# A selective scan whose reverse input terms come from TensorE instead of GpSimd

## What is computed

```python
def selective_scan(u, delta, A, Bm, Cm, D):
    def step(h, inp):
        u_t, d_t, B_t, C_t = inp
        dA = jnp.exp(d_t[..., None] * A)                       # 128 channels x 16 states
        h = dA * h + (d_t * u_t)[..., None] * B_t[:, None, :]
        y = jnp.einsum('bdn,bn->bd', h, C_t)
        return (h, y)
    ...
def run_bidir(seq, p):
    f = mamba(seq, p)
    r = jnp.flip(mamba(jnp.flip(seq, 1), p), 1)
    return 0.5 * (f + r)
```

## Time and profile before

| | |
|---|---|
| median of 3 runs | 27766.99 us (27764.99 to 27772.45) |
| the profiled execution | 27768.75 us, its span 27767.2 us |
| busy, TensorE (PE) | 18178.2 us, 65% |
| busy, VectorE (DVE) | 25925.0 us, 93% |
| busy, ScalarE (ACT) | 16996.5 us, 61% |
| busy, GpSimd (POOL) | 25520.0 us, 92% |
| DMA queue q1 | 57.9% of 16 engines' span |
| granted TensorE clock, mean | 0.81 |

### The profile page before, as it was taken

How to read it: one execution, slowest core, us unless ns; L and a number is a source line. 1 busy time by engine, 2 the same in 40 slices (tenths; PEclk the granted TensorE clock), 3 DMA queues, 4 the chain that set the end, 5 groups by cost and what they waited for, 6 DMA issues and landing times. The chain is left out here.

```text
span 27767.2 us, 284715 instructions
## 1 busy us (share of the span) xinstructions
PE 18178.2 (65%) x62778; PEld 5277.9 (19%) x62778; DVE 25925.0 (93%) x24107; ACT 16996.5 (61%) x23653; POOL 25520.0 (92%) x11268
## 2 busy tenths in 40 slices
PE   6666666666666666666666666666666666666572
PEld 1111111111111111111111111111111111111120
DVE  8999999999999999999999999999999999999321
ACT  6666666666666666666666666666666666665232
POOL 8999999999999999999999999999999999999000
PEclk8888888888888888888888888888888888887786
DMA  5555555555555555555555555555555555555967
GB/s 189 202 200 202 200 201 199 200 199 199 200 202 200 202 199 201 200 200 200 199 201 201 201 200 200 201 200 200 200 198 202 200 202 201 201 200 183 188 130 180
DMA packets 1914996, 5473.26 MB, mean 197 GB/s; under 512 B 214002, under 2 KB 642818, under 8 KB 1901458
## 3 DMA queue, kind: packets, MB, share of 16 engines
q1 hardware_dynamic: 1912968, 5451.83, 57.9%
HBM read 4644.92 MB, written 805.60 MB: 196 GB/s over the span
## 5 line engine op out<-in xcount | busy, mean ns | idle before, releaser
L796 POOL TENSOR_TENSOR drive<-du_rep,b_rep 128x1024 f32<-128x1024 f32 x8192 | 19201.4, 2389 | 114.5 <-DMA b_rep<-bc_spread 75.1
L729 DVE TENSOR_TENSOR_SCAN decay<-decay,drive 128x512 f32<-128x512 f32 x10752 | 12658.3, 1218 | 132.9 <-issue 54.6
L599 ACT ACTIVATE decay<-delta_rep,a_neg 128x1016 f32<-128x1016 f32 x8192 | 8999.1, 1106 | 598.4 <-DMA delta_rep<-delta_spread 593.6
L453 PE MATMUL y_bank<-read,sel_f 128*32 128x512 f32 x32768 | 5510.3, 805 | 2702.1 <-DVE gated L751 1798.0
L742 DVE TENSOR_TENSOR read<-decay,c_rep 128x1024 f32<-128x1024 f32 (+1 forms) x5632 | 6528.0, 1159 | 0.0
L729 DVE TENSOR_TENSOR_SCAN state<-decay,drive 128x512 f32<-128x512 f32 x5120 | 6203.7, 1212 | 83.8 <-ACT decay L599 81.3
L809 POOL TENSOR_TENSOR read<-state,c_rep 128x1024 f32<-128x1024 f32 x2560 | 6099.0, 2382 | 0.0
L595 ACT COPY decay<-zeros 128x8 f32<-128x8 f32 x5632 | 946.8, 168 | 6807.3 <-DVE read L742 6626.3
L430 PE MATMUL p_bank<-e_one,sel_f 128*128 128x512 f32 x2048 | 1563.5, 854 | 2769.4 <-ACT e_one L580 2487.2
L407 PE MATMUL p_bank<-xt,taps 128*128 128x512 f32 x4096 | 2069.2, 627 | 950.1 <-ACT u L538 492.0
L453 PEld LDWEIGHTS y_bank<-read,sel_f 128*32 128x32 f32 x32768 | 1076.1, 131 | 6474.4 <-issue 4959.4
(11 more groups left out here) (109 smaller groups left out, 14419.8 us busy)
## 6 DMA issues: line engine op xcount, KB each, us to landing
du_rep<-du_spread SPq DMA_DIRECT2D x2048, 512.0 KB, 6.4
delta_rep<-delta_spread SPq DMA_DIRECT2D x2048, 512.0 KB, 6.2
b_rep<-bc_spread SPq DMA_DIRECT2D x2048, 512.0 KB, 7.7
c_rep<-bc_spread SPq DMA_DIRECT2D x2048, 512.0 KB, 4.1
du_spread<-e_log SPq DMA_DIRECT2D x512, 512.0 KB, 2.7
delta_spread<-e_one SPq DMA_DIRECT2D x512, 512.0 KB, 3.6
xt<-in_xs SPq DMA_DIRECT2D x1024, 128.0 KB, 3.4
bc_spread<-bc SPq DMA_DIRECT2D x1024, 64.0 KB, 1.6
```

What stands on the lines that cost most here:

```text
L453: mm = nc.tensor.matmul(y_bank[32 * j:32 * j + 32, :], gather, read[:, (ROW * m + j) % READ_RING, px(d)], start=(m == 0 and d == FWD), sto ...
L599: nc.scalar.activation(inner(place[:, :]), inner(delta_rep[:, j, :]), ACT.Exp, scale=a_neg[s][:, ROW * j + m:ROW * j + m + 1]).then_inc(s_ ...
L729: nc.vector.tensor_tensor_scan(to[:, ::step], decay[place_of(turn, h, q)][:, px(d)][:, ::step], drive[:, q % DRIVE_RING, px(d)][:, ::step] ...
L796: nc.gpsimd.tensor_tensor(drive[:, q % DRIVE_RING, :], du_rep[h][:, j, :], b_rep[:, m, :], ALU.mult).then_inc(s_drive, 1)
```

## The change

The scan of a direction now has its own layout and its own instructions.

- A unit has 16 slots of 1024 columns: eight forward (F) and eight reverse (R), in turn. F slot f covers two channel groups j of one state group m, 512 positions each. R slot r covers 32 channels on the partitions 32g to 32g+31 for four groups g of states, and its columns are (2 sequences, 4 states m, 128 positions); four R slots make one half ("pair") of the sequences.
- The scan of a slot is one VectorE instruction of 1024 columns.
- F drives stay on GpSimd (eight of 1024 columns). R drives are made by TensorE: du is transposed (`turn_du`, step "tr") so that positions lie on the partitions, and is the stationary operand; the moving operand is `b_diag`, a matrix with b of position t in the columns of t and zero elsewhere, so the product gives du[c, t] * b[t, n]. Each drive is one small matmul and 16 matmuls of 64 rows x 32 columns with 256 moving columns. The moving operand is read 4 states at a time out of 16, position by position, and the output has position outermost and m innermost, with 128 elements (512 bytes) between neighbours.
- `b_diag` comes from an image in DRAM whose rows are zeros but for the 16 states in the middle (`store_b_cols`, rows of 64 bytes, from the new step "bt"); reading it with a row step of one row less 16 elements gives the diagonal blocks (`load_diag`).
- R reads (h * C) are all made by GpSimd, in place in `read_r`; VectorE makes 11 and GpSimd 5 of the 16 F reads of a tile.
- ScalarE makes an F decay in two instructions of 508 columns, and the R decays as 16 instructions of 508 columns into SBUF (`decay_r`). A place in PSUM is reused after three slots: a drive of TensorE into one waits for the F read two slots before.
- The p_bank steps are 11 instead of 9, and their places in the unit are new. The sums are four of F and two of R (`sum_r`, 16 matmuls of 256 columns each).

The diff, cut to what sets the work and its order:

```diff
-BY_POOL = (1, 4, 7, 10, 13)
-DRIVE_RING, READ_RING, STATE_RING = 4, 8, 2
+F_OPS = R_OPS = 8
+SLOTS = F_OPS + R_OPS
+WINDOW = 64
+F_BY_POOL = ((1, 5), (1, 4, 7))
+PLACES, DRIVE_RING, F_RING, R_RING = 3, 3, 4, 6
+DRIVE_AHEAD = 2
...
-STEPS = [Step("ds", FWD, 1, 0, 2), Step("ds", REV, 1, 3, 5), Step("bc", 0, 1, 6, 6),
-         Step("x", FWD, 2, 6, 7), Step("x", REV, 2, 7, 8), Step("z", 0, 1, 8, 9),
-         Step("dt", FWD, 2, 9, 10), Step("dt", REV, 2, 10, 11), Step("out", 0, -1, 12, 13)]
+STEPS = [Step("bt", REV, 1, 0, 1), Step("ds", FWD, 1, 1, 2), Step("ds", REV, 1, 3, 4),
+         Step("tr", REV, 1, 7, 7), Step("bc", 0, 1, 7, 8),
+         Step("x", FWD, 2, 8, 9), Step("x", REV, 2, 8, 9), Step("z", 0, 1, 9, 10),
+         Step("dt", FWD, 2, 10, 11), Step("dt", REV, 2, 11, 12), Step("out", 0, -1, 13, 14)]
+DU = {FWD: 3, REV: 6}
+GATE, UD = 5, 7
+R_DECAYS = {0: (4, 5), 1: (6, 7), 2: (8,), 3: (9, 10, 11), 4: (12,), 5: (13, 14, 15)}
+F_SUMS = {6: 0, 8: 1, 12: 2}
+F_SUM_LAST, R_SUM_LAST, R_SUM = 2, 3, 10
...
+            def make_drive(U, i, h, turn, r):          # TensorE
+                to = place[place_of(turn, h, 2 * r + 1)]
+                ti, th, f = before_f(i, h, r)
+                if not (isinstance(ti, int) and ti < 0):
+                    if f in F_BY_POOL[th]:
+                        pe.wait_ge(s_state, F_OPS * U + r)
+                    else:
+                        pe.wait_ge(s_read_v, read_by_vector(ti, th, f) + 1)
...
+                nc.tensor.matmul(to[0:32, 0:NS], du_cols[h][:, 2 * pair, 32 * j:32 * j + 32],
+                                 b_diag[:, pair, 0, 0:NS], start=True, stop=True, tile_position=(0, 0),
+                                 skip_group_check=True)
+                for half in range(2):
+                    for row in range(2):
+                        rows = slice(WINDOW * row, WINDOW * row + WINDOW)
+                        diag = b_diag[rows, pair, half, :].rearrange("p (t n) -> p t n", n=NS)
+                        part = to[:, px(row)].rearrange("p (m t) -> p t m", m=ROW)
+                        part = part[:, WINDOW * half:WINDOW * half + WINDOW, :]
+                        for g in range(4):
+                            mm = nc.tensor.matmul(part[32 * g:32 * g + 32, :, :],
+                                                  du_cols[h][rows, 2 * pair + half, 32 * j:32 * j + 32],
+                                                  diag[:, :, 4 * g:4 * g + 4], start=True, stop=True,
+                                                  tile_position=(WINDOW * row, 32 * g),
+                                                  skip_group_check=True)
+                mm.then_inc(s_drive_r, 1)
...
+                    for n in range(SLOTS):             # TensorE's order in a unit
+                        if n % 2 == 1 and n < SLOTS - 1:
+                            make_drive(U, i, h, turn, n // 2 + 1)
...
+                        for s, _, free, _ in rows:
+                            if s.pe == n and s.kind != "x" and n <= UD:
+                                fill(s, free, U, i, h, prev, w_prev, w_next, w_next2)
+                        if n in F_SUMS:
+                            sum_row(U, i, h, F_SUMS[n])
+                        if n == R_SUM:
+                            sum_r(U, h, turn, 0)
+                        if n == UD:
+                            add_ud(h, cur)
+                        for s, _, free, _ in rows:
+                            if s.pe == n and not (s.kind != "x" and n <= UD):
+                                fill(s, free, U, i, h, prev, w_prev, w_next, w_next2)
...
+            def scan_r(U, h, r, turn):                 # VectorE
+                if r < ROW:
+                    dve.wait_ge(s_decay_r, ROW * U + r + 1)
+                dve.wait_ge(s_drive_r, R_OPS * U + r + 1)
+                at_least(dve, s_ysum_r, 2 * U + (r - R_RING) // ROW + 1)
+                nc.vector.tensor_tensor_scan(read_r[:, r_slot(turn, h, r), :][:, ::-1], r_decay(r),
+                                             place[place_of(turn, h, 2 * r + 1)][:, ::-1], 0.0,
+                                             ALU.mult, ALU.add).then_inc(s_state_r, 1)
```

More of the change, by code:

```diff
@@ L57, in at_least, with state_of, place_of, drive_slot @@
     engine.wait_ge(semaphore, value)
[L60 to L90, removed]
+def state_of(m, g):
+    return 4 * g + m
+def place_of(turn, h, n):
+    return (2 * SLOTS * turn + SLOTS * h + n) % PLACES
+def drive_slot(turn, h, f):
+    return (2 * F_OPS * turn + F_OPS * h + f) % DRIVE_RING
+def r_slot(turn, h, r):
+    return (2 * R_OPS * turn + R_OPS * h + r) % R_RING
+def read_by_gpsimd(i, h, f):
+    return (len(F_BY_POOL[0]) + len(F_BY_POOL[1])) * i + len(F_BY_POOL[0]) * h \
+        + sum(1 for n in F_BY_POOL[h] if n < f)
+def read_by_vector(i, h, f):
+    per = [F_OPS - len(s) for s in F_BY_POOL]
+    return (per[0] + per[1]) * i + per[0] * h + sum(1 for n in range(f) if n not in F_BY_POOL[h])
 class Step:
@@ L452, in sum_row, with sum_r @@
+            def sum_r(U, h, turn, pair):
+                pe.wait_ge(s_read_r, R_OPS * U + ROW * pair + ROW)
+                part = slice(2 * SIDE * pair, 2 * SIDE * pair + 2 * SIDE)
+                for m in range(ROW):
                     for j in range(ROW):
-                        mm = nc.tensor.matmul(y_bank[32 * j:32 * j + 32, :], gather,
-                                              read[:, (ROW * m + j) % READ_RING, px(d)],
-                                              start=(m == 0 and d == FWD), stop=(m == 3 and d == REV),
+                        slot = read_r[:, r_slot(turn, h, ROW * pair + j), :]
+                        slot = slot.rearrange("p (s m t) -> p s m t", s=2, m=ROW)
+                        mm = nc.tensor.matmul(y_bank[32 * j:32 * j + 32, part], gather[1], slot[:, :, m, :],
+                                              start=False, stop=(m == 3 and pair == 1),
@@ L625, in _ @@
             for d in range(2):
[L626 removed]
+                act.wait_ge(s_proj, 13 + d)
                 take_dt(d, 0)
             for part in range(4):
[L629 to L631 removed]
+                softplus(1, part, 17)
+            act.wait_ge(s_image, 16 * 8)
+            for n in range(ROW):
+                make_decay_r(0, 0, n)
+            make_decay(0, 0, 0, 0, 0)
             def take(s, use, before, U, h, w_prev, w_next, w_next2):
@@ L829, in _ @@
-            over_tiles(pool, body, lambda i: None)
+                    for f in range(F_OPS):
+                        if f > 0:
+                            read_r_state(U, h, f - 1, turn)
+                        elif not (prev is None and h == 0):
+                            read_r_state(U - 1, 1 - h, R_OPS - 1, turn if h == 1 else (turn - 1) % PLACES)
+                        ahead = f + DRIVE_AHEAD
+                        if ahead < F_OPS:
+                            make_drive(U, h, i, ahead, turn)
+                        elif w_next is not None:
+                            make_drive(U + 1, 1 - h, i + h, ahead - F_OPS, (turn + h) % PLACES)
+                        if f in F_BY_POOL[h]:
+                            read_f_state(U, h, f)
@@ L1534 @@
         arrays[f"out_t_{s}"] = w["out_w"].T
-        arrays[f"a_log_{s}"] = w["A_log"].reshape(ROW, 32, ROW, 4).transpose(1, 3, 0, 2).reshape(P, PAIRS)
+        a = w["A_log"].reshape(ROW, 32, NS)
+        forward = a.reshape(ROW, 32, ROW, 4).transpose(1, 3, 0, 2).reshape(P, NS)
+        order = np.array([[state_of(m, g) for m in range(ROW)] for g in range(4)])
+        reverse = a[:, :, order].transpose(2, 1, 0, 3).reshape(P, NS)
+        arrays[f"a_log_{s}"] = np.concatenate([forward, reverse], 1)
         arrays[f"cols_{s}"] = np.stack([w["conv_b"], w["dt_b"], w["D"]], 1)
```

509 lines of the change are left out of this document (320 added, 189 removed).

## The result

The changed kernel takes **29911.36 us** (median of 4 runs, 29903.37 to 29922.45). The kernel before takes 27769.72 us on the same chip (4 runs, 27764.99 to 27773.44). The ratio is **1.077, 95% interval 1.075 to 1.079**: 2142 us slower, where 240 us faster was forecast. Over 512 units that is 54.11 us a unit against 49.93; of the 35 us that the prediction adds for the prologue, 12 came (the first scan starts at 89.6 us instead of 78.0), and what follows the last scan takes 2131 us, where it took 2132.

The account below looks back on a forecast made before the run. GpSimd and VectorE were taken as full before. After: VectorE's 43.1 us plus waits of 3.7, 0.5 and 0.4 is 47.7, with low clock 49.4 us a unit; with 35 us of prologue about 27530 us, range 26650 to 29600.

Parts of the forecast that it names:

- the prologue: Start of the kernel: zeroing the DRAM images, 8.3 MB, takes 40 us once, part under other work; 35 us added.
- What bounds the kernel before: Scan stage: GpSimd (99.7% busy) and VectorE (99.1%) are both full, GpSimd a little fuller; 49.93 us a unit.
- The engines' own work: Work a unit after the change: GpSimd 42.9 us, VectorE 43.1, ScalarE some 35, TensorE about 44.
- The drive: TensorE's R drive: 16 matmuls in 8 tiles run together, 0.86 us plus about 0.3, so 1.2 us each.
- A drive of twice the length: Twice the array time a drive adds 1.7 us to the chain; a busier TensorE keeps its clock: 49 to 50 us.
- The chain: TensorE's steps from drive 4 to drive 5, mid-unit: 13.0 us at full clock, so R5 waits a mean 3.7 us.
- The wait for du: VectorE waits for du some 0.5 us as ScalarE is late to the b columns, plus 0.4 for the clock.
- DMA: Transfers in the steady state: cost nothing while the chain holds, up to 1 us if a load lands late.
- a wait of VectorE for ScalarE's decays: Sign against the account: if VectorE waits for ScalarE's decays, the prediction's account is wrong.
- Slow steps: Rival: drives' strided PSUM writes and operand reads slow the matmuls; against the change from about 2.3 times; chance 0.18.
- Hidden chain: Rival: du turning and convolutions overlap better, so VectorE and GpSimd set the end: 43.5 to 46 us; chance 0.10.
- The low clock: Rival: TensorE's chain begins at half clock in most units, 50.1 to 52.5 us, 27850 to 29100 us; chance 0.29.

Follow-up runs that it names:

- early chain: The changed kernel with the reverse du, its turning, the forward convolution and the b columns' copy one slot earlier: 28235.88 us.
- the order alone: The changed kernel with only SyncE's order new: b_diag loads issued early, then b, and delta ahead of c; 28447.65 us.
- the fastest version: The changed kernel with both the early chain and the new order of loads: 26803.96 us, 0.9651 times the kernel before.

## Why the prediction was wrong

**What bounds the kernel before**: stood. **The engines' own work**: stood. GpSimd 42.9 forecast, 43.1 measured; ScalarE 35 and 35.1; TensorE 44 and 42.6; a scan of 1024 columns 2.2 and 2.2 (VectorE's timeline has one at 11999.08 and the next instruction at 12001.27). VectorE has 43.9 instead of 43.1. The prediction costed every instruction by its pitch, but one that is followed by a wait is busy for its whole record: a scan 2.28 us instead of 2.19, a read 1.23 instead of 1.14. There are nine such places in a unit, which makes 0.8. Reads cost another 0.57 of idle time: each now follows its own scan directly and waits 0.13 us for it, which the order before had not shown.

**The drive**: stood, 0.16 and 1.09 us where 1.2 was forecast. The Trainium skill, "PSUM — Partial Sum Buffer", Specifications (TRN2), has any non-contiguous pattern slow matmuls significantly, and I gave that 0.18. For fp32, with 512 bytes between neighbours in the output, no run here shows it, and the measurement decides: 5134.3 us against 5146.8 with unit steps. A drive of twice the length was foreseen to cost little, since a busier TensorE keeps more of its clock; with all drives doubled the kernel took 255 us less.

**The chain**: the mechanism stood, and nearly its size on R5, 4.61 us with the clock's share against 5.0. One reading in it was wrong: in the units of h = 1 VectorE has no read 4 to do while the chain runs, but it has read 5; in the units of h = 0 it is the other way round (`F_BY_POOL`). So R5's wait at full clock was 3.1 us in both kinds of unit, not 3.1 and 4.2, and the two kinds measured alike (4.69 and 4.52 us); with that the sum on R5 is 4.4 us. The unit shown has 15.8 us from drive 4 to R5 instead of 13.0, nearly all of the excess in the steps that ran at a granted 0.50 to 0.67. The early chain shows that it could have been avoided at no cost of work.

**The wait for du** is the first term that failed: 0.9 forecast, 3.04 measured, 2.1 us a unit. The prediction saw that ScalarE comes late to the b columns, but costed the sum behind them as if the clock were full, and took 0.4 for the clock. That sum lost 2.2 us a unit by its clock, and had done so before the change, where VectorE didn't stand still for it. Three of its four matmul pairs took 2.07, 1.91 and 1.88 us in the unit shown instead of 1.13, 1.02 and 1.02: 2.7 us. The b columns take 1.04 us there instead of 0.3 (mean 0.91). The care about the clock had gone to the middle of the unit alone.

**DMA** is the second, and it is a step that failed, not a size. "Nothing while the chain holds" was argued from an average (57% of 49.9 us) and from the time between issue and use of the diagonal blocks and of b. I didn't lay the some 40 transfers of a unit on a time axis. There they fill the engines for 28 us on end, and delta, which ScalarE needs first in the next unit, is issued behind 23 others (from 12019.40 on), with five after it. That is F0's 1.45 us, part of the wait for du and part of R5's: by the order alone 2.9 us a unit (1464 / 512).

Put together: 2.1 (du) + 1.45 (F0) + 0.57 (reads) + 0.8 (busy) + 0.26 (other) less 0.5 (R5, R6 and F6) is 4.7 us a unit, 54.1 against 49.4. The prediction had itself named a wait of VectorE for ScalarE's decays as a sign that its account is wrong; F0's is that wait (705.6 us, while ScalarE waits for delta).

**The rivals.** Slow steps: out. Hidden chain: out for this kernel; the fastest version has a unit of 48.0. The low clock came nearest: its price, up to 52.5 us a unit, was right in sign and too small, since it was placed in the chain alone. (The 51.5 us that the prediction has as the end of a quarter at low clock throughout comes out of none of its terms.) The prediction allowed up to 1 us for a late load and no rival had one, so the range's upper end, set by the slow steps, fell short by 311 us.

What stays open: why packets of 4096 bytes take a mean of 270 ns in the changed kernel (nearly four of five belong to loads of `b_diag`) and took 183 before, whether by the rows in DRAM or by what runs beside them. No run separates them. R5's remaining 1.12 us and the forward du's 1.11 in the fastest kernel were not followed up.

## What to carry to other kernels

When work moves off two full engines, the next bound need not be an engine's sum: lay the order of one unit out, transfers included, and ask which load is issued last and needed first. An average DMA share of 57% or 70% says nothing on that; the stretch in which it is 1.00 does. And where TensorE's short steps gate another engine, cost them at the clock of the stretch they fall in.

## What the runs showed of the hardware beyond that

- More TensorE work made this kernel faster. Two drives made twice: 29911 to 29263 us, mean granted clock 0.846 to 0.902; all eight: 29656 us at 0.928. It didn't pay where little of the wait for the sum was left (26804 to 26999 us in the fastest kernel).
- Sixteen fp32 matmuls of 64 rows, 32 columns and 256 moving columns, eight at a time, take 1.09 us from first to last at full clock. "Eight at a time" is worked out: one after another the 32 records of 0.215 us would take 6.9 us, in fours 1.7. Steps in PSUM and in the moving operand together made no difference (5134.3 and 5146.8 us).
- A VectorE read placed directly behind the scan that it reads waits 0.13 us for it (the scan of 12038.60 ends at 12040.87, its read starts at 12041.00).
